# Small matmuls of the mixer stage, sent to the tiles of the array in another order

## The reference, cut to what matters

```
sw  = softmax((xm @ W_slice.T + b_slice) / temp)          # 40 nodes x 64 slices
st  = einsum('bhnc,bhng->bhgc', fx, sw) / (sw.sum(2) + 1e-5)
ot  = hydra(st)          # in-projection, convolution, scan over 64 steps both ways,
                         # B.C products, gate, rms norm, out-projection
out = einsum('bhgc,bhng->bhnc', ot, sw) @ out_w.T + out_b
```

## Time and profile before

| | |
|---|---|
| median of 3 runs | 3127.1 us |
| profiled execution, span from first to last instruction | 3331.1 us |
| PE matmul records | 2524.9 us busy, 18840 records |
| DVE | 2094.1 us busy |
| ACT | 1309.8 us busy |
| POOL | 721.2 us busy |
| mixer stage in the span | about 159 to 1493 us, 16 chunks |

### The profile page before, as it was taken

The page is one execution under the profiler, slowest core; times in us unless marked ns, Lnnn a source line. Parts: engine busy times, 40 slices in busy tenths (PEclk is TensorE's granted clock), DMA queues, the critical chain, the costliest instruction groups (busy, mean ns, idle before and its releaser), DMA issues. The chain is left out here.

```text
span 3331.1 us, 50319 instructions
## 1 busy us (share of the span) xinstructions
PE 2524.9 (76%) x18840; PEld 1620.7 (49%) x18840; DVE 2094.1 (63%) x4114; ACT 1309.8 (39%) x2407; POOL 721.2 (22%) x756
## 2 busy tenths in 40 slices
PE   6477999999999999965566178587649989971542
PEld 5334555555555555545255167344326666641542
DVE  6737787778788878856646397654743547761212
ACT  4333444444444444424555004232224444451431
POOL 0000000000000000010064630166610033306244
PEclk7688999999999999987689557698879978885766
DMA  4431112222221121113223101000012221111333
GB/s 76 130 107 42 49 49 49 55 60 53 50 49 49 49 49 49 46 40 121 67 77 75 43 17 18 13 5 5 5 32 70 52 50 41 41 33 56 94 87 93
DMA packets 189058, 178.78 MB, mean 54 GB/s; under 512 B 83700, under 2 KB 162177, under 8 KB 185977
## 3 DMA queue, kind: packets, MB, share of 16 engines
q1 hardware_dynamic: 168064, 137.00, 16.5%
q0 software_dynamic: 20768, 38.75, 4.8%
HBM read 139.11 MB, written 43.64 MB: 55 GB/s over the span
## 5 line engine op out<-in xcount | busy, mean ns | idle before, releaser
L3557 PE MATMUL hy_ps<-hy_uT,hy_win 128*128 128x512 f32 x1152 | 499.3, 594 | 0.0
L3557 PEld LDWEIGHTS hy_ps<-hy_uT,hy_win 128*128 128x128 f32 x1152 | 217.9, 190 | 283.0 <-issue 272.2
L2469 POOL DMA_DIRECT2D ek_w<-ek_src x32 | 17.8, 556 | 1162.6 <-DVE ek_dst L2491 1162.6
L3619 PE MATMUL hy_ps<-hy_wo,hy_yg 128*128 128x512 f32 x512 | 239.6, 613 | 14.5 <-ACT XNP L3762 8.7
L3055 PE MATMUL er_c<-XNG 128*128 128x400 f32 x480 | 184.0, 540 | 0.0
L3619 PEld LDWEIGHTS hy_ps<-hy_wo,hy_yg 128*128 128x128 f32 x512 | 94.2, 193 | 125.6 <-issue 99.3
L2690 PE MATMUL f_px<-XNG 128*128 128x40 bf16 x736 | 69.0, 266 | 98.2 <-DVE XNG L2605 66.0
L3841 DVE TENSOR_TENSOR_SCAN XNG<-XNG,hy_fx 128x2048 f32<-128x2048 f32 x32 | 141.6, 4425 | 3.0 <-issue 0.4
L2988 POOL DMA_INDIRECT er_gone<-er_nodes,er_sidx x120 | 123.7, 1031 | 36.6 <-issue 36.3
L3055 PEld LDWEIGHTS er_c<-XNG 128*128 128x128 f32 x480 | 97.6, 209 | 69.5 <-issue 14.5
L946 DVE TENSOR_TENSOR f_hg<-f_hs,f_gb 128x640 f32<-128x640 f32 x64 | 52.7, 825 | 109.9 <-ACT f_hs L928 91.3
(11 more groups left out here) (698 smaller groups left out, 6123.4 us busy)
## 6 DMA issues: line engine op xcount, KB each, us to landing
XNG<-hy_decays SPq DMA_DIRECT2D x32, 1024.0 KB
hy_rb<-hy_inverse SPq DMA_DIRECT2D x128, 128.0 KB, 3.5
f_gb<-gate_rows SPq DMA_DIRECT2D x16, 640.0 KB, 5.1
g_KB<-g_keys SPq DMA_DIRECT2D x32, 320.0 KB
f_xg<-f_rows SPq DMA_DIRECT2D x54, 128.0 KB
f_ys<-f_ysl SPq DMA_DIRECT2D x54, 128.0 KB
f_y<-f_ysl SPq DMA_DIRECT2D x47, 128.0 KB
f_rows<-in_x_dram POOLq DMA_DIRECT2D x2, 2560.0 KB, 16.0
```

The lines of the kernel that those rows point to most:

```text
L3557: mm = pe.matmul(p[:], win[:, t, m * 128:(m + 1) * 128], uT[:, t, :], start=(t == 0), stop=(t == KT - 1))
L3619: mm = pe.matmul(PS[4 + q % 2][:], yg[:, t, q * 128:(q + 1) * 128], wo[:, t, :], start=(t == 0), stop=(t == KT - 1))
```

## The change

A list `CORNERS` gives the order (j, head) in which the heads pair up over both graphs: (0,0), (0,1), (1,0), (1,1), (0,2), ... so that successive matmuls take the four corners in turn. Before, a block did the 8 heads of one graph and then those of the other. `slices`, `mix` and `back_to_nodes` use it. In `slice_sums` the loop over q is now the outer one, so that the four column groups come in turn. In `gains` the 8 products of 64 rows come first and the 4 of 128 rows behind them.

```diff
+        CORNERS = [(j, 2 * k + a) for k in range(SH_ // 2) for j in range(2) for a in range(2)]
...
             def slice_sums(k):
...
-                for par in range(2):
-                    for f in range(2):
-                        o = PS[6][32 * (2 * par + f):32 * (2 * par + f + 1), 0:2 * SG].rearrange("p (k n) -> p k n", k=2)
-                        for q in range(CHP):
+                for q in range(CHP):
+                    for par in range(2):
+                        for f in range(2):
+                            o = PS[6][32 * (2 * par + f):32 * (2 * par + f + 1), 0:2 * SG].rearrange("p (k n) -> p k n", k=2)
                             rhs = sw[:, q, :].rearrange("p (f k a n) -> p f a k n", f=2, a=2, n=SG)[:, f, par]
                             mm = pe.matmul(o, selS[:, q, :], rhs, start=(q == 0), stop=(q == CHP - 1))
...
             def slices(k):
...
-                        for j in range(2):
-                            for h in range(SH_):
-                                o = place(q) + (h // 2) * SG
-                                mm = pe.matmul(PS[2 * (q % 2) + j][half(h % 2), o:o + SG], fx[rows(j), q, h * 64:(h + 1) * 64],
-                                               sw[rows(j), q, h * 64:(h + 1) * 64], start=True, stop=True)
+                        for j, h in CORNERS:
+                            o = place(q) + (h // 2) * SG
+                            mm = pe.matmul(PS[2 * (q % 2) + j][half(h % 2), o:o + SG], fx[rows(j), q, h * 64:(h + 1) * 64],
+                                           sw[rows(j), q, h * 64:(h + 1) * 64], start=True, stop=True)
...
             def gains(k):
...
                         pe.matmul(PS[7][half(j), q * SEQ:(q + 1) * SEQ], xs[0:64, KT, b], Cs[:, b], start=True, stop=True)
+                for q in range(CHP):
                     pe.matmul(PS[7][:, 256 + 8 * q:264 + 8 * q], xs[:, KT - 1, q * 128:(q + 1) * 128], wfd[:, KT - 1, :], start=True, stop=True)
```

More of the change, by code:

```diff
@@ L3596, in mix @@
                 for q in range(CHP):
[L3597 to L3601, removed]
+                    for j, h in CORNERS:
+                        o = (h // 2) * 128 + (q % 2) * SEQ
+                        mm = pe.matmul(PS[2 * (q // 2) + j][half(h % 2), o:o + SEQ], xt[half(j), q, h * 64:(h + 1) * 64],
+                                       W[half(j), h, q, :], start=True, stop=True)
                     if q % 2:
@@ L3627, in back_to_nodes @@
                     for q in pair:
[L3628 to L3632, removed]
+                        for j, h in CORNERS:
+                            o = place(q) + (h // 2) * N
+                            mm = pe.matmul(PS[2 * (q % 2) + j][half(h % 2), o:o + N], ot[half(j), q, h * 64:(h + 1) * 64],
+                                           swT[half(j), par, q, h, :], start=True, stop=True)
                     mm.then_inc(s["o_ps"], 1)
```

## The result

The changed kernel takes 3109.19 us (median of 9 runs, 3089.29 to 3119.64) against 3128.98 us of the kernel before in the same session (9 runs, 3117.44 to 3140.49). The ratio of the two is 0.9927, 95% interval 0.9903 to 0.9951, so it is really faster: by 20 us or 0.6% between the medians, by 0.7% in the ratio. That is two thirds of the 30 us forecast. It lies inside the wide range (3079 to 3125) and on the side of "within 1%", but outside the forecast's own 3089 to 3106; taken alone, the time is nearer to rival 1 (3112) than to the forecast (3097). The profile has to tell which of them it was.

What follows compares the result with a forecast made beforehand. DVE's chain was taken to bound each turn's first half, PE the second. 1.7 us over 14 turns (23.8), plus 4.4 and 1.6 at the ends, gave 29.8 us: 3127.1 to 3097, own range 3089 to 3106, wide range 3079 to 3125.

Steps and rivals of the forecast that it cites:

- rival 1: Slice sums: only two column groups work at once, saving 0.53 us there; 15 us in all, 3112; chance 0.13.
- rivals 1 and 2: The second: interleaving column groups of the same rows gains nothing in the slice sums; 7 us in all, 3120; chance 0.08.
- rival 5: Whole kernel: the hardware already takes tiles out of order and nothing changes; 3127 us; chance 0.04.
- Slice sums, 1.38 on the path: Slice sums on PE fall from 2.46 to 1.08 us, all 1.38 saved on the path each turn.
- Slices, "worth 0": Slice products save 0.65 us on PE, but PE then waits longer for DVE before L3560; worth 0.
- Gains, 0.22: Gains save 0.73 us on PE, but ACT's exponentials can come forward only some 0.22; worth 0.22 a turn.
- Return to nodes, 0.1 of 0.45: Return to nodes saves 0.45 us on PE; POOL's table and transfers come forward less, so worth 0.1.
- The ends: Outside the 14 steady turns: 4.4 us in the first two slice sums, 1.6 us in the last two chunks.
- All savings on the path (54 us): Rival: DVE's chain follows PE, so all block savings, 3.86 us a turn, reach the end; 3067 us; chance 0.08.
- A price for each switch of the tile: Rival: every switch of the row half costs time, blocks take 3.6 us; slower, 3177 us; chance 0.07.
- theories A to C: From the experiments: A, longer wait lowers clock, out waits for POOL; B, POOL's round alone; C, slices, mix or gains useless.

Runs made afterwards that it cites:

- e4: The changed kernel with the slices back in their old order and POOL's table of places made early, before the round of transfers; 3089.22 us.
- e11: The kernel before with slice sums and gains reordered, POOL's table made early and the corner order in back_to_nodes alone; 3086.14 us, ratio 0.9868.
- e1: The changed kernel with the slices back in their old order; 3100.98 us.
- e3: The changed kernel with POOL's table for the next edge-key piece made before the round of transfers, not behind it; 3099.84 us.
- e5: The kernel before with only the slice sums reordered; 3115.54 us, ratio 0.9955.
- e2: The changed kernel with one superfluous matmul, its result overwritten, put into PE's wait before L3560; 3109.66 us.
- e7: The kernel before with only the gains grouped by shape; 3124.13 us, ratio 0.9993.
- e9: The kernel before with slice sums and gains reordered, all 64-matmul blocks in the old order; 3099.70 us, ratio 0.9900.
- e10: The kernel before with slice sums and gains reordered and POOL's table made early; 3096.92 us, ratio 0.9890.
- e6_corners: The kernel before with only the corner order in slices, mix and back_to_nodes; 3137.01 us, ratio 1.0017.
- e8: The kernel before with only POOL's table made early; 3115.93 us, ratio 0.9971.

## Why the prediction was right, and where not

The quiet parts add up edit by edit: 78.47 less 1.38 (slice sums), 0.25 (gains), 0.45 (return to nodes), and nothing for slices and mix, is 76.4, and 76.38 was measured after. So the prices of the edits were right. What was left out is the clock, and the lag was sized a little low. That the time still fell into 3079 to 3125 is owed to the width of that range, which holds rivals 1 and 2 as well, and to nothing that the forecast said of the clock: in that respect it is luck. (The range leaves out rival 5, too, at 3127, which the prediction does not say.)

- **The bound.** Right. DVE's chain sets the first half of the turn, PE the second. Reordering slices and mix moved no end: e4 and e11, with and without the mix, have the same turn, and after and e1, with and without the slices, the same quiet part. The waits on PE grew instead, as forecast: 0.29 to 0.93 (e4), 0.73 to 1.38 (e3), and 0.61 to 1.08 before L3619.
- **Size of the blocks.** Right: forecast 2.1, 2.1, 2.05, 1.08 and 1.5 us, measured 2.09, 2.10, 2.08, 1.08 and 1.53. The four column groups do run together, 12 records in flight against six at the old seams. The rule of the Trainium skill that was weighed there ("TensorE: Matmul & The Clock Gate", Part 3, The mechanism), that weight loads overlap matmuls in flight only where the row group differs, would, as the prediction read it, have left the slice sums at 2.46 us; the 1.08 us measured decide against it for these column groups.
- **Slice sums, 1.38 on the path.** Right. The wait ahead of them is 0.84 us as before, and the quiet part fell by 1.39 in e5. By themselves they brought less (e5: 77.89), for the reason in the next but one point.
- **Slices, "worth 0".** This is the step that failed. The sum let the wait before L3560 grow to 1.4 us and costed a wait of PE at nothing, because DVE ends it. After the change 6 spells in 12 turns began where that wait ends, and the stretch from `out` to L3640 was 9 us longer over the twelve than in e2, e4 and e11, which have none. e1 and e4, which shorten the wait, have 1 and none; e2, which fills it, has none. This term was not 0 but about -0.75 us a turn. With it and the lag below, 76.8 + 0.75 + 0.1 is 77.65 of the 77.70 measured. (The saving of 1.02 is counted from 78.72, a mean that holds the one spell of before, 1.70 / 12 = 0.14.) The longer wait is not the slices' alone: the lag lengthens it as well.
- **Gains, 0.22.** Right as a term (0.25, e7 and e9), and incomplete. Beside quicker slice sums they also keep the spells behind the old gains away: e5 to e9, 77.89 to 76.96. Of that 0.93 the forecast had 0.22; the rest is the spells.
- **Return to nodes, 0.1 of 0.45.** Right in its mechanism: POOL's table and the round of transfers ahead of it became what `out` waits for. The mean lag at the ends of the turns is 0.51, 0.47 above that of an undisturbed turn, so that the term was about 0 rather than 0.1; with the table early, all 0.45 come through (quiet part 76.83 to 76.38, e10 to e11). And the lag had a second effect that was not foreseen: it lengthens the very wait before L3560 behind which the clock falls. With the lag gone, the profile of e3 had one spell instead of six; its other runs may have had more (above), so that how much of the spells is owed to the lag is not shown.
- **The ends.** Right: 4.3 us in the first two slice sums against 4.4.
- **The rivals.** Two column groups at a time, and none, fall with 12 records in flight and 1.08 us. All savings on the path (54 us) falls with e4 against e11 and with the waits, which grew as forecast. A price for each switch of the tile falls with blocks of 2.1 us, not 3.6. Nothing changes falls with all of them. e6_corners shows, though, that there was another way to come out slower, to which the prediction gave no rival: not by the matmuls themselves, but by the clock behind them.

Of theories A to C, A holds for the spells, with the addition of the second place behind the gains. B is right that POOL's round holds the turn up in part, by 0.47 us, but not alone: the spells' 0.75 lie ahead of the end of L3640, where the lag has no part. C falls for slice sums, gains and return to nodes; it holds for the mix (worth nothing) and the slices (worth less than nothing).

**What stays open.** Why one wait brings a spell and another doesn't. In the changed kernel waits of 1.67, 1.72, 1.92, 1.94, 2.37 and 2.63 us did, while 1.80, 1.86 and 2.12, and all of 1.60 or less, did not; in e1 one of 2.59 did not and one of 2.63 did; in e2 ten waits of 1.76 or 1.77 us behind the inserted matmul never did. Nor is it shown why gains of 2.25 us, with no wait, brought spells in five of twelve turns once the slice sums were shorter, and in one before that. Also open are the longer transfer round of e2_fill, how many spells e3 has in an ordinary run, and where and why e8 loses less to the clock.

## What to carry to other kernels

Issue small matmuls of different corners or column groups in turn where the block stands on the path; where another engine ends the wait behind it, nothing is won by it, and the longer wait can cost clock: price PE's idle time by the granted clock behind every wait that a change lengthens. Read a turn in two parts, up to the end of the engine that should set it and the lag behind that, since an experiment can mend one and harm the other, as e2_fill did. When an edit brings an engine forward, find the queue that was just in time before (here POOL's table behind its transfers) and move its cheap instruction ahead of the slow ones. Time the parts of a change apart: here three of its five edits were worth having, and these alone, with the early table, took 41 us off where the whole took 20 (each against the kernel before of its own set).

## What the runs showed of the hardware

- Four 32-column groups of the same 128 rows work at once: 12 records in flight, 32 records in 1.08 us against 2.46 (L3520). 128 records on four 64x64 corners, sent in turn, took 2.09 us, 16 in flight, against 2.74 with eight matmuls (16 records) of one graph together (L3534).
- In the changed kernel the granted clock fell to the 1.2 GHz level at the end of waits of 1.67 to 2.63 us (L3560), in 6 of 12 turns, and was back at 2.4 GHz 3.4 us later; in e6_corners it did so in 4 of 12, at 1.69 to 2.58 us. Other waits as long brought nothing. Each time PE lost 1.4 to 1.7 us.
- It also falls with no wait ahead, behind 2.25 us of small products whose shape changes eight times: the 5.38 us of L3619 in e5_sums, against 3.68. Grouped by shape (1.53 us), they were followed by no such spell in the twelve turns of after, e1 to e4, e7 and e9 to e11; with the old order before, e5 and e6 had 1, 5 and 4, and e8 none.
